# A gated delta rule layer with a SwiGLU feed-forward: SyncE's transfers placed in parts, five engine lists in a new order

## What is computed

```python
x_act = jnp.tanh(x); static_out = einsum('bld,ed->ble', x_act, W)      # q = k = x_act in 16 heads of 16, v = static_out
# per head:  S = lam*S;  u = beta*(v_t - S^T k_t);  S = S + k_t u^T;  o_t = S^T q_t
y = static_out + o;   y = (y - mu) * rsqrt(var + 1e-5) * ln_gamma + ln_beta
x = layernorm(x + y)
gate, up = x @ wg.T, x @ wu.T                # 256 -> 768, int32 weights / 127
x = layernorm(x + (silu(gate) * up) @ wd.T)  # 768 -> 256
```

## Time and profile before

| | us |
|---|---|
| median of 3 runs | 1710.55 |
| lowest, highest | 1705.41, 1717.15 |
| the profiled execution's own time | 1699.24 |
| its span | 1697.4 |
| mean granted TensorE clock | 0.881 |

### The profile page before, as it was taken

The page is one execution under the profiler, slowest core; times in us unless marked ns, Lnnn a source line. Parts: engine busy times, 40 slices in busy tenths (PEclk is TensorE's granted clock), DMA queues, the critical chain, the costliest instruction groups (busy, mean ns, idle before and its releaser), DMA issues.

```text
span 1697.4 us, 53741 instructions
## 1 busy us (share of the span) xinstructions
PE 1362.5 (80%) x21032; PEld 1062.5 (63%) x21032; DVE 1352.3 (80%) x3461; ACT 1115.9 (66%) x2357; POOL 842.8 (50%) x1106
## 2 busy tenths in 40 slices
PE   4357888888888888888888888887888888888764
PEld 3345676666666666666666666666666666666542
DVE  5588888888888888888888888888788788888841
ACT  3335777667767776676777677766667677676544
POOL 6124455555544655454455555445555544555542
PEclk9557889989989998898899899898999899899877
DMA  4556445565655555566455566654565555455200
GB/s 121 118 109 119 106 122 121 119 124 114 130 118 120 122 122 116 114 123 130 110 120 119 120 125 117 125 116 115 115 116 121 114 131 117 118 117 120 52 23 25
DMA packets 701325, 190.98 MB, mean 113 GB/s; under 512 B 620944, under 2 KB 688528, under 8 KB 701072
## 3 DMA queue, kind: packets, MB, share of 16 engines
q1 hardware_dynamic: 701072, 187.56, 52.1%
HBM read 103.55 MB, written 67.11 MB: 101 GB/s over the span
## 4 chain that ended last, share of the span: by engine, by line
DVE 29%; SPq 18%; PE 16%; DMA 13%; issue 12%; ACT 8%; POOL 4%; ACTq 0%; POOLq 0%; DVEq 0%
SPq L1059 8%; DMA xa<-L_attn_x 6%; PE pc L182 6%; DMA scr_g<-gs 5%; PE pg L253 4%; DVE tt L451 4%; SPq L1072 4%; PE pu L253 4%; DVE gs L443 3%; DVE gate L495 3%; SPq L994 3%; DVE xt L406 2%; DVE x1lo L488 2%; DVE U L382 2%; DVE R L377 2%
## 5 line engine op out<-in xcount | busy, mean ns | idle before, releaser
L953 POOL TENSOR_TENSOR hlo<-gate,hhi 128x512 f16<-128x512 f32 x192 | 264.0, 1385 | 357.0 <-ACT hhi L783 354.9
L182 PE MATMUL pc<-R,tb 128*128 128x32 f16 x4096 | 158.1, 186 | 119.3 <-DVE R L372 117.3
L182 PEld LDWEIGHTS pc<-R,tb 128*128 128x128 f16 x4096 | 146.7, 118 | 139.8 <-DVE R L372 137.7
L182 PE MATMUL pc<-U,kb 128*128 128x32 f16 x4096 | 158.9, 188 | 85.3 <-DVE U L382 85.1
L182 PEld LDWEIGHTS pc<-U,kb 128*128 128x128 f16 x4096 | 146.9, 118 | 114.7 <-DVE U L382 114.6
L182 PEld LDWEIGHTS pc<-S,e 128*128 128x128 f16 x4096 | 150.1, 118 | 67.9 <-DVE S L399 64.4
L182 PE MATMUL pc<-S,e 128*128 128x32 f16 x4096 | 157.1, 186 | 41.5 <-DVE S L399 41.4
L279 PE MATMUL pd<-wd_t,hhi 128*128 128x256 f16 x768 | 174.5, 274 | 7.5 <-POOL hlo L953 5.1
L279 PE MATMUL pd<-wd_t,hlo 128*128 128x256 f16 x768 | 174.1, 274 | 0.0
L216 PEld LDWEIGHTS pf<-xb,e 128*128 128x128 f16 x4096 | 153.8, 118 | 31.5 <-DMA e<-scr_x 16.3
L216 PE MATMUL pf<-xb,e 128*128 128x32 f16 x4096 | 156.3, 191 | 17.5 <-DMA e<-scr_x 15.9
(11 more groups left out here) (132 smaller groups left out, 3222.4 us busy)
## 6 DMA issues: line engine op xcount, KB each, us to landing
xa<-L_attn_x SPq DMA_DIRECT2D x128, 128.0 KB
scr_x<-xt SPq DMA_DIRECT2D x64, 256.0 KB, 2.1
xb<-scr_x SPq DMA_DIRECT2D x256, 64.0 KB, 2.9
e<-scr_x SPq DMA_DIRECT2D x256, 64.0 KB, 3.7
scr_g<-gs SPq DMA_DIRECT2D x32, 512.0 KB, 3.5
gh<-scr_g SPq DMA_DIRECT2D x32, 512.0 KB, 3.3
kb<-k SPq DMA_DIRECT2D x512, 32.0 KB, 2.3
scr_t<-t SPq DMA_DIRECT2D x64, 256.0 KB, 3.6
```

The lines of the kernel that those rows point to most:

```text
L182: last = pe.matmul(pc2[:, :, cols], stationary(h, a), moving[:, :, cols], start=a == 0, stop=a == 1)
L953: pool.tensor_tensor(hlo[:, t, :], gate[:, t % 2, :], hhi[:, t, :], ALU.subtract).then_inc(SEM["hl"], 1)
```

## The change

All arithmetic, all DMAs and all buffers stay. SP's helpers get a range (`batches` or `chunks`), so that the eight or four DMAs of one transfer can stand at several places in the list; the waits are in the first part alone. Each of the five lists is written anew, and each starts at another point of the ring of operations (hence `s + 1`, `s + 2` for `s - 1`, `s`, and `FIRST, LAST = -5, NS + 1`); how many steps of the sequence are in flight between an engine's first and last operation does not change. ACT's first variance waits for the fourth variance of the step before in addition.

```diff
-        FIRST, LAST = -3, NS + 3
+        FIRST, LAST = -5, NS + 1
...
             if n == 0:
                 act.wait_ge(SEM[f"mq{z}"], n_of(f"mq{z}", q))
+                if z == 2:
+                    act.wait_ge(SEM["va3"], n_of("va3", q - 1))
...
-        def sp_load_inverse(sp, q, p, g):
-            if q == 0:
+        def sp_load_inverse(sp, q, p, g, batches):
+            if q == 0 and batches[0] == 0:
...
+            if batches[0] == 0:
+                sp.wait_ge(SEM[f"td{g}"], n_of(f"td{g}", q))
+                sp.sem_inc(s_hop, 1)
+                sp.wait_ge(SEM["tp"], n_of("tp", q - 1, 2 * g + 2))
+            for b in batches:
```

PE's list around the Gram products, and its static products in the recurrence:

```diff
-            if live(s - 2):
-                pe_gate(pe, s - 2, p, 4)
-                pe_up(pe, s - 2, p, 3)
-                pe_up(pe, s - 2, p, 4)
-            if live(s + 1):
-                pe_gram(pe, s + 1, 1 - p, 0, range(0, 8))
-                pe_gram(pe, s + 1, 1 - p, 0, range(8, 16))
-                pe_gram(pe, s + 1, 1 - p, 1, range(0, 8))
-                pe_gram(pe, s + 1, 1 - p, 1, range(8, 16))
-            if live(s - 2):
-                pe_gate(pe, s - 2, p, 5)
...
+            if live(s):
+                pe_up(pe, s, p, 3)
+                pe_gate(pe, s, p, 4)
+                pe_up(pe, s, p, 4)
+                pe_gate(pe, s, p, 5)
+            if live(s + 3):
+                pe_gram(pe, s + 3, 1 - p, 0, range(0, 8))
+                pe_gram(pe, s + 3, 1 - p, 0, range(8, 16))
+            if live(s):
+                pe_up(pe, s, p, 5)
...
+            if live(s + 2):
+                pe_keys_by_update(pe, s + 2, p, 1)
+                pe_keys_by_state(pe, s + 2, p, 2)
+            if live(s + 3):
+                pe_static_out(pe, s + 3, 1 - p, 2)
+            if live(s + 2):
+                pe_inverse_by_rest(pe, s + 2, p, 2)
+            if live(s + 3):
+                pe_static_out(pe, s + 3, 1 - p, 3)
+            if live(s + 2):
+                pe_keys_by_update(pe, s + 2, p, 2)
```

More of the change, by code:

```diff
@@ new lines, in dve_step @@
+            if live(s + 1):
+                dve_state_high(dve, s + 1, 1 - p, 2)
+                dve_state_sum(dve, s + 1, 1 - p, 2)
+            if live(s + 2):
+                dve_invert_scale(dve, s + 2, p, 5)
+            if live(s + 1):
+                dve_state_low(dve, s + 1, 1 - p, 2)
+            if live(s + 2):
+                dve_invert_add(dve, s + 2, p, 5)
+            if later(s + 3):
+                dve_transpose_keys(dve, s + 3, 1 - p, 0)
+                dve_transpose_keys(dve, s + 3, 1 - p, 1)
@@ new lines, in act_step @@
+            if live(s):
+                act_variance(act, s, p, 2, 1)
+                act_variance(act, s, p, 2, 2)
+            if later(s + 3):
+                act_activate(act, s + 3, 1 - p)
+            if live(s):
+                act_variance(act, s, p, 2, 3)
+            if live(s + 2):
+                act_static_out(act, s + 2, p, 0)
+                act_static_out(act, s + 2, p, 1)
+            if live(s + 1):
+                act_state(act, s + 1, 1 - p, 2)
+            if later(s + 3):
+                act_transpose_keys(act, s + 3, 1 - p, 0)
+                act_transpose_keys(act, s + 3, 1 - p, 1)
@@ L1108, in sp_step @@
[L1108 to L1116 removed]
+            if live(s + 3):
+                sp_load_inverse(sp, s + 3, 1 - p, 1, range(4, 6))
+            if later(s + 5):
+                sp_load_x(sp, s + 5, 1 - p, range(0, 2))
+                sp_load_x(sp, s + 5, 1 - p, range(2, 4))
@@ new lines, in sp_step @@
+            if live(s + 4):
+                sp_load_kb(sp, s + 4, p, 0, range(4, 6))
+                sp_load_kb(sp, s + 4, p, 0, range(6, 8))
+            if later(s + 5):
+                sp_store_keys(sp, s + 5, 1 - p, 0)
+                sp_store_keys(sp, s + 5, 1 - p, 1)
+                sp_spread_packed_keys(sp, s + 5, 1 - p, range(0, 2))
+                sp_spread_keys(sp, s + 5, 1 - p, range(0, 2))
+                sp_spread_keys(sp, s + 5, 1 - p, range(2, 4))
+            if live(s + 3):
+                sp_load_residual(sp, s + 3, 1 - p, range(0, 2))
@@ new lines, in sp_step @@
+            if later(s + 5):
+                sp_spread_keys(sp, s + 5, 1 - p, range(4, 6))
+                sp_spread_packed_keys(sp, s + 5, 1 - p, range(2, 4))
+                sp_spread_packed_keys(sp, s + 5, 1 - p, range(4, 6))
+            if live(s + 4):
+                sp_store_inverse(sp, s + 4, p, 0)
+            if later(s + 5):
+                sp_spread_keys(sp, s + 5, 1 - p, range(6, 8))
+                sp_spread_packed_keys(sp, s + 5, 1 - p, range(6, 8))
+            if live(s + 3):
+                sp_load_residual(sp, s + 3, 1 - p, range(2, 4))
@@ L1119, in all_steps @@
+            if live(s + 5):
+                sp_store_gram(sp, s + 5, 1 - p)
+            if live(s + 4):
+                sp_store_inverse(sp, s + 4, p, 1)
+            if live(s + 5):
+                sp_load_gram(sp, s + 5, 1 - p)
+            if live(s + 4):
+                sp_load_inverse(sp, s + 4, p, 1, range(0, 2))
+                sp_load_inverse(sp, s + 4, p, 1, range(2, 4))
         def all_steps(eng, step):
```

697 lines of the change are left out of this document (332 added, 365 removed).

## The result

| | before | changed |
|---|---|---|
| median of 5 runs, us | 1710.55 | 1726.53 |
| lowest, highest | 1705.41, 1717.15 | 1722.42, 1729.65 |
| the profiled execution: own time, span | 1699.24, 1697.4 | 1722.42, 1720.5 |
| mean granted clock | 0.881 | 0.861 |

The ratio is 1.0091 (95% interval 1.0058 to 1.0123): 16 us slower. That is clear of the noise; the median lies within the 1% that was called "no change", and the interval reaches a little beyond it. The forecast was 1719 us, the range 1688 to 1743.

A forecast was written before the change was run, and what follows sets the result against it. No engine is full; a ring of waits through each 49.14 us step bounds the kernel. Terms -0.58 + 0.7 + 0.3 - 0.1 = +0.3 us, times about 30 steps, +9 us on 1710.55: 1719 us, range 1688 to 1743.

The forecast's parts named there:

- Within 1%: Whole kernel: the change cannot be told from no change, 17 us either way; chance 0.44.
- x in time (-0.58): ACT, tanh behind `U`: the wait for x no longer delays `U`, -0.58 us per step.
- SP, after the Gram store: SP's list: two inverse loads issued behind x, so x comes 0.98 us earlier; cost by itself 0.
- The text on DMAs: Gram and inverse stores in flight together: stores could delay x, some +0.1 us on average, sum then 1722 us.
- State copy and transposes (+0.7): Behind `U`: the tanh in ACT's list makes state copy and key transposes late, +0.7 us per step.
- +0.3, if the transposes run at the fast clock: Lower bound, in us per step, of the term for the late state copy and key transposes behind `U`.
- PE and DVE around the Gram products (+0.3): Early sixth gate product waits for ACT, last Gram pass on DVE moves later: +0.3 us per step.
- rival (a): Feed-forward half: PE stands before the sixth gate product in every step, +0.8 us per step, 1735 us; chance 0.24.
- Keys and inverse (-0.1): SP's key spreads, inverse store and loads: later spreads against fewer waits, together -0.1 us per step.
- rival (d): Gram products on PE wait 0.5 us per step for late key spreads, +24 us, 1735 us; chance 0.10.
- Rival (b): PE's clock stays up at transposes and feed-forward start, -0.75 us per step, 1688 us; chance 0.14.
- Rival (c): Only the load of x matters and little else moves: -15 us, 1695 us; chance 0.14.

The follow-up runs named there:

- a1: The changed kernel with the last two of the eight inverse loads ahead of the loads of x again: 1704.96 us, ratio 0.9969 to the kernel before.
- a2: The changed kernel with ACT's third window in the old order, tanh ahead of `U`: 1708.8 us, ratio 0.9998 to the kernel before.
- d1: The kernel of a1 with ACT's second variance moved ahead of `U`: 1698.2 us, ratio 0.9949 to the kernel before.
- b1: The kernel before with the tanh behind `U` and two of the variances, SP's list old: 1707.95 us, ratio 0.9992.
- a3: The changed kernel with DVE's fourth Gram pass ahead of the two feed-forward adds again: 1713.3 us, ratio 1.0015 to the kernel before.
- b2: The kernel before with the sixth gate product ahead of all Gram products, nothing else: 1750.51 us, ratio 1.0253.
- d2: The kernel of d1 with DVE's fourth Gram pass also ahead of the two feed-forward adds: 1694.21 us, ratio 0.9928 to the kernel before.
- d4: The kernel of a1 with PE's third and fourth static products in their old places: 1711.07 us, ratio 1.0033 to the kernel before.
- e2: The kernel of d2 with the sixth gate product behind the first Gram piece: 1700.47 us, ratio 0.9961 to the kernel before.
- b5: The kernel of b1 with PE's third and fourth static products in the changed kernel's places: 1704.32 us, ratio 0.9964 to the kernel before.
- b4: The kernel before with only the last two of the eight inverse loads moved behind the loads of x: 1692.79 us, ratio 0.9917.

## Why the prediction was right, and where it was not

"Within 1%" and the sign held, the time lies in the range, and 1719 against 1726.5 us is near. The nearness is in part luck: the sum left out one term of 0.6 us per step, and part of that was offset by terms taken too dear.

- **x in time (-0.58): the mechanism right, the gain not had.** ACT's wait for x went from 18.7 to 1.0 us. But the step "SP, after the Gram store" counted that x is issued 0.98 us earlier and never what the two loads moved behind it lose: 2.66 us of x's issuing. The same `U` waits for them, through PE's third inverse product. The window lost 0.65 us to x before and loses 0.63 us to the inverse after. Measured by a1, this missing term is +21 us. The text on DMAs weighed completion order against a slack of x, and the load that was late was the other one. Its +0.1 us for x did not come (one wait, of 1.0 us), and its inference that a store issued behind the Gram store can hold that one up does not show: the load of the Gram matrices follows the store by 3.6 us, before by 3.8.
- **State copy and transposes (+0.7): right, at the lower side.** `U` to the copy was to go from 3.13 to 3.7 us; it is 3.14 and 3.66. The piece behind `U` grew by 0.46 us. The next one grew by 0.14, but it is 6.29 to 6.32 us in all kernels with the new lists, a2 and d1 with their early copy too, so that part is not this term's. The bound "+0.3, if the transposes run at the fast clock" named the cause of the difference: b1 at the low clock pays 1.0 us.
- **PE and DVE around the Gram products (+0.3): too dear, and right in sum only with the next term's loss.** The piece up to the update product grew by 0.21 us, but 0.16 of that stands in four steps in which PE waited for `e` (next term), which leaves 0.05. Behind it the first state sum comes 0.31 us later, 0.17 of it by the place of the Gram pass (a3), and 0.27 us comes back in the next two pieces. The weight load waits 17.5 us for ACT's gate tile in 45 cases, 0.4 us each, and PE nearly never. The price that rival (a) feared exists, and alone it is larger than I put it (b2, 1.5 us per step); by the traces DVE's and POOL's new lists had paid it off before PE came there, which no run tests. I had held that the two `hlo` come no earlier.
- **Keys and inverse (-0.1): a small loss in place of a gain.** After the Gram store its load follows 3.6 us later on average (before 3.8). The second inverse store, put at 0, cost nothing: the first inverse load follows the Gram store by 4.2 us (before 4.3). But behind the start-up PE's weight load waits for the key spread `e` four more times, at 368, 1019, 1119 and 1366 us, 0.9 to 1.6 us each and 4.9 us in all; before, it is one wait of 0.2 us. These four steps raise the mean of their piece by 0.16 us. a1, a3, d1, d2, d4 and e2 have three to seven such waits, 3.8 to 7.3 us, as well, a2 one of 0.5 us. So rival (d)'s mechanism is there at about a third of its 0.5 us per step; which of the moves in SP's list brings it was not tested.
- **Rival (b), the clock.** The transposes did run at full clock in most steps (eight in under 1.3 us in 19 of 27, before in 5). The stretch that answers to the one at 782 in the earlier trace rows, and two feed-forward starts:

```profile
core 0: us, PE busy (x) PEld busy (x) DVE busy (x) ACT busy (x) POOL busy (x), PEclk, DMA share, GB/s
996.00:1000.00 4.00, 2.77 (x53) 2.45 (x54) 3.57 (x11) 3.98 (x10) 2.00 (x5) 0.90 0.41 97
858.00:862.00 4.00, 3.76 (x10) 1.34 (x10) 3.12 (x11) 0.10 (x1) 0.00 (x0) 0.50 0.60 113
1007.00:1011.00 4.00, 3.77 (x18) 1.69 (x19) 3.67 (x12) 1.58 (x3) 0.00 (x0) 1.00 0.65 127
```

The clock at the transposes is 0.90 in this step and was 0.50. At the feed-forward's start both levels still occur, and that piece has not moved (6.60 and 6.56 us), so the larger part of rival (b)'s gain did not come. The static products lengthened from 282 to 327 ns each, because the low stretch now stands at the third and fourth of them. That is not why the mean clock fell: as medians of the runs, the new places raise it (d4 0.862, a1 0.8745; b1 0.8625, b5 0.872). It falls with the tanh behind `U` (0.877 before, 0.8625 in b1) and with the late inverse loads (a1 0.8745, changed 0.864).
- **Rival (c)** needs the copy not to move; it moved.

Had the late loads been seen, the forecast would have been the sum with -0.58 replaced by about 0: +0.9 us per step, 27 us, 1737 us. So the other terms were too dear together, by 0.4 us per step going by the medians and by 0.1 going by the two profiles.

## What to carry to other kernels

When a load is moved ahead of others in one queue, write down for each of the others when it is issued now, when it lands and which product waits for it: here two loads that the same `U` waits for simply exchanged places as the one that is late. Take the time to landing from rows in which the same transfers stand ahead; it was 1.7 us without x ahead and 3.0 us behind it. A reordering of one engine's list has a price only together with the lists beside it: an early product that cost 2.5% alone cost little in the changed lists. If work is put behind the critical step of a window, look at what stands between it and the next one, and at the clock level at which that runs.

## What the runs showed of the hardware

- The last 32 KB load of the inverse landed 1.6 to 1.8 us behind the end of its issue as a mean over the steps in the ten kernels in which other inverse loads alone stand just ahead of it (1.74 in the kernel before, 1.68 in a1), and 2.9 to 3.0 us in the four in which the four 128 KB loads of x do (changed 3.00, b4 2.92). Being moved behind x cost it 2.6 to 2.8 us of issuing and 1.2 to 1.3 us of landing.
- Of the static products, 1 us each, the third and the fourth were moved one place down, so that one stands between the third window's inverse and update product. With this the eight transposes some 2 us later took 1.06 us in place of 1.94 in 17 to 19 of 27 steps (changed, a1, b5), against 0 to 5 (d4, b1, before); in d1 and d2, where the transposes also come earlier, in all 27. The stretch at 0.50 moved to the products ahead.
- The feed-forward's start did not react to that move. It takes 6.05 to 6.08 us on average in the steps at full clock, in every kernel, and 8.0 to 8.3 us at a mean clock of 0.73 to 0.75; how many steps begin low changed from kernel to kernel (means of 6.44 to 6.90 us) with no order that I can name, and this alone hides gains of 0.4 us per step in a single profile.
